# Loads of all lower result parts ahead of group 1's higher part, on the scatters' own semaphores, and TensorE's additions in the order lower parts, then higher parts

## The chip, the cores and the metric

The kernel runs on one core of one Trainium2 chip. The metric is the device time in microseconds (us) of one execution; several executions are timed, and their median is compared. One more execution was taken with the hardware profiler, and all rows below come from it. In what follows SP is the engine that only issues transfers and waits, POOL is GpSimd, DVE is VectorE, ACT is ScalarE and PE is TensorE.

## The reference, cut to what matters

Input `x` has 16 sequences of 256 tokens of 128 numbers: 4096 tokens, 32 tiles of 128 tokens. Two blocks follow each other, each `x = x + s * silu(ffn(xn))`, with `xn = layernorm(x)` and `s` the result of an attention-like layer. Only the end of the second block is touched here:

```
logits = xn @ Wg;  P = softmax(logits);  the two best of 8 experts are kept
h   = gelu(xn @ W1[e] + b1[e])            # 128 -> 512, per expert e
y_e = h @ W2[e] + b2[e]                   # 512 -> 128
y   = sum over the two experts of y_e * P_norm[e]
x   = x + s * silu(y)
```

So each token has two expert results. The one of its expert with the lower number is called its lower part, the other its higher part; `y` is their sum.

## The kernel before, in words

**Groups and units.** The tokens are worked on in 8 groups (0 to 7) of 512. For the second block's experts the rows are routed: POOL scatters every normalised token twice to the DRAM tensor `routed`, sorted by expert, and units of 256 rows of one expert are then read back and multiplied. The first 8 units are the first of each expert (`FIRST_ALL`); the others follow expert by expert, from 0 to 7, in `other_units`. How many there are depends on the data: DVE writes the bounds to `table`, a small row of whole numbers on the chip, and every engine reads them from there (`value_load`, shown in the trace as TENSOR_LOAD with register work behind it). With the reference's inputs the experts get 1096, 830, 727, 1419, 1359, 728, 1148 and 885 rows, which makes 36 units, numbered u0 to u35 here. Expert 6 has its other units in u29 to u32 and expert 7 in u33 to u35.

**What a unit does.** PE turns the unit's rows (L1067), multiplies by W1 (L1077), ACT applies gelu (L1286), PE multiplies by W2 (L1089), DVE adds the bias (L1692), copies the destination rows and weights (L1699, L1702) and multiplies by the weights (L1708). POOL then scatters the 256 result rows in two halves (`scatter`, L739) to the DRAM tensor `results`. There a token's lower part lies in the first 4096 rows and its higher part in the next 4096. The scatters of even units count up the semaphore `y_sent0`, those of odd ones `y_sent1`, by 16 for each half as it lands. In `send_results` POOL issues the first half of unit u, waits until unit u-1 has landed whole (`tell_landing`), counts up `y_landed` (L746), and issues the second half of u. Two others wait for `y_landed`: DVE before it copies the destination rows of unit u (all up to u-2 must have landed), and SP below.

**The end of the kernel on SP.** When the ring of units is loaded, SP reads the results back in 16 loads of 256 KB (`load_results`, L596; 512 tokens by 128 numbers of 4 bytes): 8 lower parts to `res_lower[g]` and 8 higher ones to `res_higher[g]`. Both lie in SBUF room that the program knows by other names: `w_all` (the expert weights) and, for lower part 7, `nT`. Before each load SP reads from `table` how many units must have landed for it (`units_due`, L459) and waits for `y_landed`. With these inputs the numbers are: lower parts 0 to 7: 29, 30, 31, 31, 31, 32, 33, 33; higher parts 0 to 7: 29, 34, 34, 34, 35, 35, 36, 36. (31 means: u30 is the last that must have landed.) The order of the loads is: lower 0, 1, 2, 3, higher 0, 1, lower 4, 5, 6, 7, higher 2, 3, 4, 5, 6, 7. The last two wait for all scatters on `y_sent0` and `y_sent1` directly. Behind the loads, on the same queue, stand the 8 stores of the output (L621), each waiting for its group.

**The end on the other engines.** The parts of groups 0 and 1 are added by DVE (`add_parts`, L1730; `SUMS_BY_DVE = 2`): group 0 ahead of the last unit's bias, group 1 behind the last unit. The parts of groups 2 to 7 are added by PE, as products with a unit matrix that add up in PSUM: for each pair of groups first the two lower parts (L1137, each waiting for its `lower_in`), then the two higher ones (L1140, each waiting for its `res_in`). ACT applies silu group by group (L1317), DVE multiplies by `s` (L1752), adds to `x_all` (L1754), and SP stores. `surplus_results` (L1744) is one small copy that DVE makes behind group 1; it waits for `y_landed` to reach 35.

## Time and profile before

| | us |
|---|---|
| median of 3 runs (lowest, highest) | 445.61 (443.02, 446.01) |
| the profiled execution, its own time | 443.66 |
| its span from the first to the last instruction | 441.9 |
| PE busy in the span | 407.1 (92%) |
| DVE busy | 288.2 (65%) |
| ACT busy | 214.2 (48%) |
| POOL busy | 155.6 (35%) |

The profiled execution is 1.95 us below the median and inside the spread of the three runs; 1.8 us of it lie outside the span. All times below count from the start of the span. "Busy" counts the time in which an engine runs an instruction; the granted clock (PEclk) is the share of full speed that PE was given. A row of the timeline begins with its start and its duration; in square brackets stand the idle time before it and what ended it.

### The profile page before, as it was taken

Reading aid. Unit: us, or ns where it says so; the run is one execution under the profiler, and the core shown is the slowest. Engines: PE = TensorE matmul, PEld = TensorE weight load, DVE = VectorE, ACT = ScalarE, POOL = GpSimd, SP = SyncE. Lnnn points to the kernel's source line nnn. Section 1 sums busy time; section 2 is a strip of 40 time slices with the busy share of each in tenths; the row PEclk is TensorE's granted clock in tenths of the full one; section 3 lists DMA queues with packets and bytes.
Section 4 is the critical chain, followed back from the end, with each engine's and each line's share of the span. In section 5 each row is a group of like instructions: output and inputs, shape, how many; then the busy total and the mean of one; then the engine's idle time right before and its main releaser. Section 6 shows DMA issues by size and latency. Waiting matters only on the chain.

```text
span 441.9 us, 9899 instructions
## 1 busy us (share of the span) xinstructions
PE 407.1 (92%) x2936; PEld 344.5 (78%) x2936; DVE 288.2 (65%) x1149; ACT 214.2 (48%) x525; POOL 155.6 (35%) x215
## 2 busy tenths in 40 slices
PE   8699998999999999999988898889999999999845
PEld 7579777878869779887867788778999999999612
DVE  4889888888888887878866658612433333344445
ACT  3364555556554545542523354323555555555512
POOL 6340015013233250344424002344555555555510
PEclk9999999999999999999999999999999999999969
DMA  7449611244155131131131323321333222223384
GB/s 179 127 111 150 79 40 35 58 151 137 32 159 164 42 87 50 41 90 47 39 86 39 88 52 90 110 70 53 87 85 96 73 71 68 62 73 112 118 297 144
DMA packets 64210, 40.80 MB, mean 92 GB/s; under 512 B 18340, under 2 KB 57128, under 8 KB 64168
## 3 DMA queue, kind: packets, MB, share of 16 engines
q1 hardware_dynamic: 59472, 31.27, 29.5%
q0 software_dynamic: 4352, 8.99, 6.1%
q8 instruction: 21, 0.34, 0.3%
q14 instruction: 21, 0.17, 0.2%
q10 hardware_dynamic: 344, 0.03, 0.1%
HBM read 21.78 MB, written 18.48 MB: 91 GB/s over the span
## 4 chain that ended last, share of the span: by engine, by line
PE 70%; DVE 17%; ACT 5%; issue 4%; DMA 2%; SPq 1%; POOL 0%; DVEq 0%; ACTq 0%; POOLq 0%
PE psA L1077 14%; PE psC L1089 11%; PE psB L903 7%; PE psB L891 5%; PE psB L1100 2%; DVE stats L1375 2%; PE psB L1067 2%; PE psD L1020 2%; DVE nt_a L1390 1%; DVE rstd L1391 1%; DVE nt_a L1389 1%; PE psB L893 1%; PE psD L1003 1%; ACT send L1152 1%; PE psA L849 1%
## 5 line engine op out<-in xcount | busy, mean ns | idle before, releaser
L734 POOL DMA_INDIRECT routed<-send,slot x64 | 64.4, 1006 | 128.0 <-DMA routed<-send,slot 56.4
L739 POOL DMA_INDIRECT results<-nat,y_to x72 | 69.8, 970 | 85.6 <-DVE nat L1708 42.2
L1077 PE MATMUL psA<-xuT,w_all 128*128 128x256 f32 x288 | 68.6, 381 | 1.7 <-ACT h1T L1286 1.0
L1286 ACT ACTIVATE h1T<-psA,b1T 128x256 f32<-128x256 f32 x144 | 63.3, 475 | 8.9 <-PE psB L1100 7.2
L1077 PEld LDWEIGHTS psA<-xuT,w_all 128*128 128x128 f32 x288 | 50.6, 190 | 9.4 <-issue 1.9
L1089 PE MATMUL psC<-w_all,h1T 128*128 128x128 f32 x464 | 56.6, 275 | 0.6 <-ACT h1T L1286 0.6
L1089 PEld LDWEIGHTS psC<-w_all,h1T 128*128 128x128 f32 x464 | 54.1, 192 | 0.8 <-ACT h1T L1286 0.8
L1277 ACT ACTIVATE xuT<-psB 128x256 f32<-128x256 f32 x37 | 14.2, 384 | 62.2 <-PE psB L1067 62.2
L1692 DVE TENSOR_TENSOR nat<-psC,b_all 128x256 f32<-128x256 f32 x29 | 12.3, 425 | 34.3 <-PE psC L1089 34.3
L1680 DVE TENSOR_SCALAR xu<-l_room 128x256 f32 (+1 forms) x38 | 11.3, 298 | 35.7 <-PE psB L1067 25.2
L891 PE MATMUL psB<-xnT,l_room 128*128 128x512 f32 x64 | 34.3, 618 | 0.0
L1217 ACT ACTIVATE hg0T<-psB,b1T 128x512 f32<-128x512 f32 x32 | 22.0, 688 | 22.8 <-PE psB L893 22.7
L903 PE MATMUL psB<-l_room,hg0T 128*128 128x128 f32 x256 | 32.7, 281 | 0.2 <-ACT hg0T L1217 0.2
L903 PEld LDWEIGHTS psB<-l_room,hg0T 128*128 128x128 f32 x256 | 31.2, 192 | 1.1 <-ACT hg0T L1217 0.6
L893 PEld LDWEIGHTS psB<-selT,expert_of 128*128 128x128 bf16 x128 | 9.8, 98 | 18.2 <-issue 18.2
L1708 DVE TENSOR_SCALAR nat<-nat,y_wt 128x128 f32 (+1 forms) x72 | 18.3, 304 | 7.6 <-DVE y_wt L1702 7.4
L794 PE MATMUL psC<-ident 128*128 128x128 f32 x136 | 20.1, 300 | 1.7 <-POOL ident L638 1.7
L1224 ACT ACTIVATE gg<-psB,tok_w 128x128 f32<-128x128 f32 x32 | 9.2, 368 | 25.1 <-PE psB L904 25.1
L794 PEld LDWEIGHTS psC<-ident 128*128 128x128 f32 x136 | 18.6, 214 | 2.3 <-POOL ident L638 1.7
L723 POOL COPY send<-send 128x512 f32<-128x512 f32 x8 | 5.4, 671 | 41.1 <-ACT send L1152 27.9
L1375 DVE BATCH_NORM_STATS2 stats<-x_all 128x6 f32<-128x128 f32 x64 | 13.9, 279 | 5.9 <-DMA x_all<-in_L_attn_x_dram 5.8
L1152 ACT ACTIVATE send<-x_all,shift,rstd 128x128 f32<-128x128 f32 x32 | 13.2, 483 | 8.8 <-DVE shift L1392 8.7
(296 smaller groups left out, 851.9 us busy)
## 6 DMA issues: line engine op xcount, KB each, us to landing
l_room<-routed SPq DMA_DIRECT2D x38, 130.0 KB
inv<-inv_room SPq DMA_DIRECT2D x8, 512.0 KB, 4.1
w_all<-results SPq DMA_DIRECT2D x15, 256.0 KB, 3.8
routed<-blank SPq DMA_DIRECT2D x24, 130.0 KB, 7.5
n_room<-nT SPq DMA_DIRECT2D x8, 256.0 KB, 2.3
w_all<-in_L_ffn_W_dram SPq DMA_DIRECT2D x1, 2048.0 KB, 9.7
out_dram<-x_all SPq DMA_DIRECT2D x8, 256.0 KB, 2.3
results<-nat,y_to POOLq DMA_INDIRECT x72
```

The costliest lines, as they stand in the source:

```text
L734: pool.indirect_dma_start(routed[:, :], bass.IndirectOffsetOnAxis(ap=slot[par][:, c, t:t + 1], axis=0), send[par][:, c, t, :], None).then_ ...
L739: pool.indirect_dma_start(results[:, :], bass.IndirectOffsetOnAxis(ap=y_to[:, par, a:a + 1], axis=0), yw[:, par, a, :], None).then_inc(S[f ...
L794: mm(to, ident[:, :], ident[:, :], start=True, stop=True)
L891: mm(psB[:, j % 2, :], w, xT0[:, :], start=True, stop=False)
L903: mm(o, hg0T[:, j, col(t)], w2_l0[:, j, :], start=(j == 0), stop=False)
L1077: last = mm(psA[:, j // 2, (j % 2) * UNIT:(j % 2 + 1) * UNIT], w1_all[:, e, j * P:(j + 1) * P], xuT[:, :], start=True, stop=True)
L1089: last = mm(psC[:, a, 0:D], h1T[:, k, a * P:(a + 1) * P], w2_all[:, f * JF + k, :], start=(k == 0), stop=(k == JF - 1))
L1152: last = f(to[:, t, 0:D], x_all[:, g * TILES + t, :], ACT.Identity, scale=rstd[:, first + t:first + t + 1], bias=shift[:, first + t:first ...
L1217: f(hg0T[:, j, :], psB[:, j % 2, :], ACT.Gelu, bias=b1T[:, HT + j:HT + j + 1]).then_inc(S["hg0_ready"], 1)
L1286: f(h1T[:, j, :], psA[:, j // 2, (j % 2) * UNIT:(j % 2 + 1) * UNIT], ACT.Gelu, bias=b1T[:, n:n + 1]).then_inc(S["gelu_ready"], 1)
L1375: last = v.bn_stats(stats[:, first + t, :], x_all[:, x_first + t:x_first + t + 1, :])
L1708: last = v.tensor_scalar(yw[:, mine, a, :], yb[:, a:a + 1, :], y_wt[:, a:a + 1], None, ALU.mult)
```

## The change

SP now reads the due counts into registers ahead of the loads (two, then seven, then three in one go), waits for `y_sent0` and `y_sent1` themselves and no longer for POOL's `y_landed`, and issues all other loads in another order: lower 0, 1, 2, 3, higher 0, lower 4, 5, 6, 7, higher 1, 2, 3, 4, 5, 6, 7. PE adds the six lower parts of groups 2 to 7 in a row and then the six higher ones. DVE makes its surplus copy behind group 2.

```
-            last_pair = sp.value_load(table[0:1, 2 * E + 1:2 * E + 2], min_val=MIN_UNITS * E - 2,
-                                      max_val=MAX_UNITS - 1)
...
-            for g in range(groups // 2):
-                wait_on(sp, "y_landed", units_due(sp, g, 0))
+            def wait_landed(units):
+
+                sp.wait_ge(S["y_sent0"], (units + 1) // 2 * (2 * 8 * HALVES))
+                sp.wait_ge(S["y_sent1"], units // 2 * (2 * 8 * HALVES))
+
+            def load_lower(g):
+                wait_landed(low[g])
                 load_results(0, g, res_lower, lower_in)
-            for g in range(SUMS_BY_DVE):
-                wait_on(sp, "y_landed", units_due(sp, g, 1))
+
+            def load_higher(g):
+                wait_landed(high[g])
                 load_results(1, g, res_higher, res_in)
-            for g in range(groups // 2, groups - 2):
-                wait_on(sp, "y_landed", units_due(sp, g, 0))
-                load_results(0, g, res_lower, lower_in)
-            wait_on(sp, "y_landed", bounds[E - 1])
+
+            low = [units_due(sp, g, 0) for g in range(2)]
+            load_lower(0)
+            load_lower(1)
+            low += [units_due(sp, g, 0) for g in range(2, groups - 2)]
+            high = [units_due(sp, g, 1) for g in range(3)]
+            load_lower(2)
+            load_lower(3)
+            load_higher(0)
+            load_lower(4)
+            load_lower(5)
+            high += [units_due(sp, g, 1) for g in range(3, groups - 2)]
+            wait_landed(bounds[E - 1])
             for g in range(groups - 2, groups):
                 load_results(0, g, res_lower, lower_in)
-            for g in range(SUMS_BY_DVE, groups - 2):
-                wait_on(sp, "y_landed", units_due(sp, g, 1))
-                load_results(1, g, res_higher, res_in)
-
-            sp.wait_ge(S["y_sent0"], (last_pair + 2) * (8 * HALVES))
-            sp.wait_ge(S["y_sent1"], (bounds[E] // 2) * (8 * HALVES * 2))
+            for g in range(1, groups - 2):
+                load_higher(g)
+            wait_landed(bounds[E])
             for g in range(groups - 2, groups):
                 load_results(1, g, res_higher, res_in)
...
-            for g0 in range(SUMS_BY_DVE, groups, 2):
-                for g in (g0, g0 + 1):
-                    pe.wait_ge(lower_in[g], 16)
...
-                    mm(sum_ps_of(g), ident[:, :], res_lower[g], start=True, stop=False)
-                for g in (g0, g0 + 1):
-                    pe.wait_ge(res_in[g], 16)
-                    mm(sum_ps_of(g), ident[:, :], res_higher[g], start=False, stop=True).then_inc(S["sum_ps"], 1)
+            for g in range(SUMS_BY_DVE, groups):
+                pe.wait_ge(lower_in[g], 16)
...
+                mm(sum_ps_of(g), ident[:, :], res_lower[g], start=True, stop=False)
+            for g in range(SUMS_BY_DVE, groups):
+                pe.wait_ge(res_in[g], 16)
+                mm(sum_ps_of(g), ident[:, :], res_higher[g], start=False, stop=True).then_inc(S["sum_ps"], 1)
...
             for g in range(groups):
                 finish(g)
-                if g == 1:
+                if g == 2:
                     surplus_results()
```

On PE, behind the last unit's products, the instructions before are these. `lower_in2` is the semaphore of lower part 2's load, `res_in2` that of higher part 2's, and the three tiles psA, psB and psC hold the sums of groups 2 and 3, 4 and 5, and 6 and 7:

```order
L1137 MATMUL psA<-w_all,ident 128x512 [waits lower_in2]
L1137 MATMUL psA<-w_all,ident 128x512 [waits lower_in3]
L1140 MATMUL psA<-w_all,ident 128x512 [waits res_in2]
L1140 MATMUL psA<-w_all,ident 128x512 [waits res_in3]
L1134 REGISTER_ALU [waits lower_in4]
L1137 MATMUL psB<-w_all,ident 128x512 [waits xuT_ready]
L1137 MATMUL psB<-w_all,ident 128x512 [waits lower_in5]
L1140 MATMUL psB<-w_all,ident 128x512 [waits res_in4]
L1140 MATMUL psB<-w_all,ident 128x512 [waits res_in5]
L1137 MATMUL psC<-w_all,ident 128x512 [waits yb_ready,lower_in6]
L1137 MATMUL psC<-nT,ident 128x512 [waits lower_in7]
L1140 MATMUL psC<-w_all,ident 128x512 [waits res_in6]
```

And now, at the same place:

```order
L1146 MATMUL psA<-w_all,ident 128x512 [waits lower_in2]
L1146 MATMUL psA<-w_all,ident 128x512 [waits lower_in3]
L1143 REGISTER_ALU [waits lower_in4]
L1146 MATMUL psB<-w_all,ident 128x512 [waits xuT_ready]
L1146 MATMUL psB<-w_all,ident 128x512 [waits lower_in5]
L1146 MATMUL psC<-w_all,ident 128x512 [waits yb_ready,lower_in6]
L1146 MATMUL psC<-nT,ident 128x512 [waits lower_in7]
L1149 MATMUL psA<-w_all,ident 128x512 [waits res_in2]
L1149 MATMUL psA<-w_all,ident 128x512 [waits res_in3]
L1149 MATMUL psB<-w_all,ident 128x512 [waits res_in4]
L1149 MATMUL psB<-w_all,ident 128x512 [waits res_in5]
L1149 MATMUL psC<-w_all,ident 128x512 [waits res_in6]
```

The four additions of lower parts 4 to 7 have moved ahead of the wait for higher part 2. On SP, the place from the loads of lower part 6 and 7 on reads as follows before:

```order
L596 DMA w_all<-results 128x512 [waits y_landed]
L596 DMA nT<-results 128x512
L459 TENSOR_LOAD table
L459 ISA x2
L409 REGISTER_ALU
L596 DMA w_all<-results 128x512 [waits y_landed]
```

And now:

```order
L594 DMA w_all<-results 128x512 [waits y_sent1]
L594 DMA nT<-results 128x512
L599 ISA
L600 ISA [waits y_sent0]
L594 DMA w_all<-results 128x512 [waits y_sent1]
```

The first row is lower part 6, the last one higher part 2 before and higher part 1 now. The table is no longer read between two loads; two register instructions work out the two counts that are waited for.

## Rows read from the trace of the kernel before

**Rows 1.** Chain of waits near the end (start, duration, what)

```profile
420.65 0.50 POOL results L739
421.16 4.81 DMA w_all<-results
...
426.00 3.71 PE psA L1140 x4
429.71 1.72 PE psB L1137 x4
```

**Rows 2.** POOL's scatters in the timeline, second halves of u31 to u35 (start, duration, instruction)

```profile
407.60 0.97 POOL L739 DMA_INDIRECT results<-nat,y_to  x1 [1.37 <-DMA results<-nat,y_to]
...
411.88 0.97 POOL L739 DMA_INDIRECT results<-nat,y_to  x1 [1.86 <-DMA results<-nat,y_to]
...
414.92 0.97 POOL L739 DMA_INDIRECT results<-nat,y_to  x1 [0.61 <-issue]
...
417.97 0.97 POOL L739 DMA_INDIRECT results<-nat,y_to  x1 [0.30 <-issue]
...
420.65 0.97 POOL L739 DMA_INDIRECT results<-nat,y_to  x1 [0.30 <-issue]
```

**Rows 3.** POOL's announcements of landed units (L746): u31 and u35

```profile
L746 POOLq EVENT_SEMAPHORE  x1: 17/17/17, 411.1 to 411.1; - x1
...
L746 POOLq EVENT_SEMAPHORE  x1: 17/17/17, 426.2 to 426.2; - x1
```

**Rows 4.** SP's loads in the timeline: lower 1, lower 2, higher 1, lower 7, higher 2

```profile
402.49 0.33 SPq L596 DMA_DIRECT2D w_all<-results  x1
...
406.88 0.32 SPq L596 DMA_DIRECT2D w_all<-results  x1
...
417.22 0.32 SPq L596 DMA_DIRECT2D w_all<-results  x1
...
420.07 0.42 SPq L596 DMA_DIRECT2D nT<-results  x1
421.16 0.32 SPq L596 DMA_DIRECT2D w_all<-results  x1
```

**Rows 5.** Issue to landing: higher 0 (408.85), higher 1 (417.22), lower 6 and 7

```profile
DMA to landing us min/median/max: 3.3/3.3/3.3
...
DMA to landing us min/median/max: 2.7/2.7/2.7
...
DMA to landing us min/median/max: 5.1/5.2/5.2
```

**Rows 6.** Stages: start and end, length, busy PE, PEld, DVE, ACT, POOL, clock, DMA share, GB/s

```profile
416.00:417.00 1.00, 1.00 (x10) 0.93 (x9) 0.33 (x2) 0.90 (x3) 0.30 (x1) 1.00 0.20 66
...
422.50:423.00 0.50, 0.00 (x0) 0.00 (x0) 0.47 (x2) 0.00 (x0) 0.00 (x0) 0.68 0.78 299
423.00:425.00 2.00, 0.00 (x0) 0.00 (x0) 0.51 (x2) 0.00 (x0) 0.00 (x0) 0.50 0.99 371
```

**Rows 7.** PE's additions of lower parts 2 and 3, in the timeline

```profile
416.74 1.88 PE L1137 MATMUL psA<-w_all,ident 128*128 128x512 f32 x4
```

**Rows 8.** DVE and ACT: adding the parts of group 1, then groups 6 and 7, in the timeline

```profile
420.02 0.69 DVE L1730 TENSOR_TENSOR w_all<-w_all 128x512 f32<-128x512 f32 x1 [1.43 <-DMA w_all<-results]
...
436.39 0.69 DVE L1752 TENSOR_TENSOR hg0T<-s,hg0T 128x512 f32<-128x512 f32 x1 [0.69 <-ACT hg0T L1317]
436.62 0.60 ACT L1317 ACTIVATE hg0T<-psC 128x512 f32<-128x512 f32 x1 [0.26 <-PE psC L1140]
...
437.73 0.68 DVE L1752 TENSOR_TENSOR hg0T<-s,hg0T 128x512 f32<-128x512 f32 x1
438.44 0.69 DVE L1754 TENSOR_TENSOR x_all<-x_all,hg0T 128x512 f32<-128x512 f32 x1
```

**Rows 9.** DVE around the waits of u33 and u34, in the timeline

```profile
411.52 0.17 DVE L1699 TENSOR_SCALAR y_to<-l_room  x1 [0.54 <-POOLq L746]
...
414.29 0.42 DVE L1692 TENSOR_TENSOR nat<-psC,b_all 128x256 f32<-128x256 f32 x1 [1.13 <-PE psC L1089]
```

More of the change, by code:

```diff
@@ L1128, in _ @@
             other_units(pe, bounds, hid, out)
-            for g0 in range(SUMS_BY_DVE, groups, 2):
-                for g in (g0, g0 + 1):
-                    pe.wait_ge(lower_in[g], 16)
-                    if g == 4:
-                        pe.wait_ge(S["xuT_ready"], bounds[E] + 1)
-                    elif g == 6:
-                        wait_on(pe, "yb_ready", bounds[E])
-                    mm(sum_ps_of(g), ident[:, :], res_lower[g], start=True, stop=False)
-                for g in (g0, g0 + 1):
-                    pe.wait_ge(res_in[g], 16)
-                    mm(sum_ps_of(g), ident[:, :], res_higher[g], start=False, stop=True).then_inc(S["sum_ps"], 1)
+            for g in range(SUMS_BY_DVE, groups):
+                pe.wait_ge(lower_in[g], 16)
+                if g == 4:
+                    pe.wait_ge(S["xuT_ready"], bounds[E] + 1)
+                elif g == 6:
+                    wait_on(pe, "yb_ready", bounds[E])
+                mm(sum_ps_of(g), ident[:, :], res_lower[g], start=True, stop=False)
+            for g in range(SUMS_BY_DVE, groups):
+                pe.wait_ge(res_in[g], 16)
+                mm(sum_ps_of(g), ident[:, :], res_higher[g], start=False, stop=True).then_inc(S["sum_ps"], 1)
         @block.scalar
```

## The prediction

> **What bounds the kernel now.** I read the chain of waits first, from its end, because only work on it can shorten the run. Up to 415 us it is PE's unit products, which the change leaves as they are. From there it is a relay: DVE and POOL finish the last unit, POOL issues its last scatter at 420.65, SP's load of higher part 2 takes 4.81 us from 421.16, and then PE adds without a pause, 3.71 us for the four products of higher parts 2 and 3 and 1.72 us for each later pair [rows 1]. The reader should see two things. PE adds lower parts 2 and 3 from 416.74 to 418.62 [rows 7] and then stands still for 7.4 us in front of higher part 2, although lower parts 4 to 7 stand behind it in its order. And the products at 426.00 take 3.71 us where later ones take 1.72, because the granted clock fell to 0.50 (1.2 GHz) in the pause: it was still 0.68 on average in 422.5 to 423, so it fell some 4 us after the last product [rows 6].
>
> Then SP's timeline: lower part 7 is issued at 420.07 and higher part 2 at 421.16 [rows 4], yet lower 6 and 7 were due when 33 units had landed and higher part 2 at 34, which SP had seen at 417.22 when it issued higher part 1. Nine loads thus stand in a row from 417.2 on (higher 1, lower 4 to 7, higher 2 to 5), just when the last scatters have to land, and the 16 transfer engines are 0.99 busy at 371 GB/s [rows 6]. Loads take 5.1 to 5.2 us there instead of 2.7 [rows 5], and u35's second half, issued at 420.65, is announced only at 426.2 [rows 2, 3]: 5.5 us, where u33's, issued at 414.92, had moved all its data by 417.0 [rows 2, 6], 2.1 us, in a window with 66 GB/s.
>
> **Part 1: reading the counts ahead.** A read and a load together take 1.09 us (421.16 less 420.07); the load alone 0.42 [rows 4], so a read costs at most 0.67. Seven reads, 4.7 us, now stand between lower part 1 (402.49) and lower part 2 (406.88) [rows 4], in a gap of 4.4 us in which SP waited. So lower part 2 comes at about 407.6, 0.7 late, which nobody waits for: PE needs it at 416.7. Three more reads (2.0 us) stand ahead of lower part 6 and are covered by the wait for u32. In front of the last higher parts no read is left: between 0.42 and 1.09 us from load to load, and I take 0.6, nearer to 0.42, as two register instructions remain.
>
> **Part 2: the semaphores.** Waiting for the landing itself saves only what POOL was late in telling. For u33 at most 0.2 us (417.0 against 417.22). For u34, whose second half was issued at 417.97 [rows 2], the telling waits until POOL has issued u35's second half at 420.65 and comes at 421.16; direct, it is due at 420.1 with 2.1 us, or 421.5 with the 3.5 us that u31's took beside three loads (407.60 to 411.1 [rows 2, 3]). A gain of up to 1.1 for higher parts 4 and 5, which is on the path only if they are late.
>
> **Part 3: the loads moved forward.** Lower 4 and 5 move to about 409.4 and 411.5, lower 6 and 7 to about 414.4 and 415.0, when u32 has landed. Each is 256 KB, 0.7 us of all transfer engines at 371 GB/s. That is bought from the scatters now in flight there. Bounds for u33: landing at 417.0 if nothing is lost; 1.4 later if both loads are served wholly first. I take 1.0 later, nearer to the upper end because POOL itself will run some tenths later behind u31 and u32: higher part 1 at 418.0, 0.8 later than before. Its own landing is between 2.7 and 3.3 us (a load with two others close by [rows 5]); I take 3.3, since higher 2 and 3 follow within 1.2 us: 421.3.
>
> The Trainium skill, page "DMA: Bandwidth & Descriptors", section "Issuing engines are not separate DMA queues", speaks against this part: transfers started by SP and by GpSimd end up on the same 16 engines and interleave. The sum by that rule alone would give back the time of every load moved into the scatters' stretch; the rows agree so far that u31's landing took 3.5 us beside loads and u33's 2.1 without.
>
> **Part 4: PE's order.** Six lower additions in a row, 1.88/2 = 0.94 us each at most [rows 7], or 0.86 by the chain: from 416.74 to 421.9 or 422.4. Lower 7 has landed by 415.0 + 3.3. Higher part 2, issued at 418.6, lands between 3.3 and 3.6 us later, at about 422. So PE has hardly a pause, keeps 2.4 GHz, and each higher part costs 0.86 us when it lands. Off PE's path go 7.4 us of standing still, less the waits for single parts.
>
> **Part 5: what is late next.** DVE. It adds the parts of group 1 once higher part 1 has landed (before at 420.02 [rows 8]), and then owes eight groups of two instructions: 436.39 to 437.73 is 1.34 us, 437.73 to 439.13 is 1.40 [rows 8], so 1.37 each. Before, six of these eight waited for PE; now they stand in a row. The surplus copy, at nothing before because DVE was waiting anyway, is now in this row: I take 0.3, between the 0.17 us of its like [rows 9] and one instruction of 0.69. DVE starts at 421.4, 0.65 for group 1's sum, 8 x 1.37 = 11.0, 0.3: **433.3**, against 439.13. The last store and the end behind it, 2.8 us, stay.
>
> Does the last group come in time? POOL: u34's second half was issued 0.75 after u33's landing was told, u35's 2.68 later [rows 2]; so 418.8 and 421.5. At 3.5 us u35 has landed at 425.0. Higher 7 is issued at 425.5 and lands, with 3.8 (between 3.3 and 4.8), at 429.3; PE 0.86, ACT 0.60: 430.8. DVE turns to group 7 at 431.9. It fits by 1.1 us.
>
> **Sum.** 439.1 - 433.3 = 5.8 us less. The profiled execution took 443.66 (span 441.9), which makes 437.9. It lay 1.95 below the median of the runs; from the median the sum gives 439.8. I put the time between the two, at **438.8 us**, with the span of a profiled execution at 436.1.
>
> **Rivals.**
>
> A. *DVE's row, as above.* Bounds: higher part 1 neither later nor slower, DVE's end 431.9, a gain of 7.2; or all ends at their worst, higher part 1 at 418.6 and 3.6 us to land, a gain of about 4.8. Chance 0.60.
>
> B. *PE falls back to 1.2 GHz between the higher parts.* Behind higher 3 PE waits for u34 and u35, twice some 2 us. For: it fell in the pause of 7.4 us. Against: it took some 4 us of standing still. Then the four products of a pair take 3.71 us: higher 6 ends at 430.9, higher 7 at 432.7, ACT 433.3, DVE 434.7. A gain of 4.4 us, time about 440.2. Chance 0.13. The Trainium skill, page "TensorE: Matmul & The Clock Gate", section "Loop structure matters more than you think", warns of a DMA wait between matmuls in this way: by it PE would go to half its clock. The trace agrees for the one long pause; it has no pause of 2 us here to judge by.
>
> C. *The scatters pay for the loads.* Every landing from u31 to u33 stretches by 1 to 1.4 us, not only u33's; POOL waits for each, so higher part 1 comes at about 420.2 and lands at 423.5, and DVE's row of 12 us ends at 435.5; u35 at about 428 gives much the same end. A gain of 3.6 us, time 441.0. For: u31's 3.5 us. Against: the last scatter meets five loads fewer. Chance 0.15.
>
> D. *The change doesn't do what it says:* lower parts 4 to 7 still land late and PE's wait only changes its place. Against: their counts are reached by 414.4. What remains is PE's clock, a gain of some 2 us (3.71 less 1.72 [rows 1]), time 442.6. Chance 0.04.
>
> E. *Slower.* The stretch runs back into the units. DVE already waited 0.54 us for the telling of u31 (ended 411.1) at 411.52, and has 1.13 us to spare before the bias of u34 at 414.29 [rows 9]. If the landings of u31 to u35 all take 3.5 us and add what they wait for, u35 is issued 6 us later; PE's last products, 2 us late beyond the spare 1.1, follow; higher 7 lands at 434.5 plus 3, and DVE ends at 437.5 + 0.86 + 0.60 + 1.4 = 440.4, which is 1.3 us later than before: 446 us, and more if the loads behind them slow down too. It decides once a scatter's landing is stretched by over 1.1 us at u32. Against: each load is only 0.7 us. Chance 0.08.
>
> **Range and chances.** Low end: A's best case from the profiled time, 436.4. High end: C's 441.0 and, since I stand between two levels 1.9 us apart, 1.3 more: 442.3. What lies outside is E, D in part and A's luckiest tail. A measurement here tells 1% (4.5 us) from no change. Faster by over 1%: A's 0.60 and half of B, 0.66. Within: the rest of B, C, D and half of E, 0.29. Slower by over 1%: 0.05.
>
> **What would show it.** Right: lower 4 to 7 issued before 415.5; PE's six lower additions in one piece from 416.7; DVE without a gap from group 1's sum to its last instruction, 12 us; u35's second half landed in under 4.5 us; granted clock 1.00 in the higher additions. Wrong: DVE waiting for ACT at groups 6 and 7 (B, or late landings); higher part 1 issued after 418.6 (C); the bias of u34 later than 414.5 (E).

## The result and the profile after

The changed kernel takes 439.44 us (median of 8 runs, 438.9 to 441.46); the kernel before, run beside it, 445.45 us (8 runs). The ratio, which is one of means, is 0.9875, with a 95% interval of 0.9849 to 0.9901: 5.6 us faster (6.0 between the two medians). I had put the gain at 5.8 and the time at 438.8. The profiled execution took 438.9 us, its span is 437.1. Ratios, here and below, leave out slow executions, of which one chip had four (480 to 1435 us); the medians given for that chip (before 452.39) count them.

The gain is where it was looked for. PE's additions in the timeline of the changed kernel (start, duration, instruction; in brackets the idle time before it and what ended it; L1146 adds lower parts, L1149 higher parts):

```profile
418.15 1.88 PE L1146 MATMUL psA<-w_all,ident 128*128 128x512 f32 x4
419.87 1.88 PE L1146 MATMUL psB<-w_all,ident 128*128 128x512 f32 x4
421.59 1.02 PE L1146 MATMUL psC<-w_all,ident 128*128 128x512 f32 x2
422.45 1.02 PE L1146 MATMUL psC<-nT,ident 128*128 128x512 f32 x2
423.31 1.88 PE L1149 MATMUL psA<-w_all,ident 128*128 128x512 f32 x4
426.42 1.98 PE L1149 MATMUL psB<-w_all,ident 128*128 128x512 f32 x4 [1.23 <-DMA w_all<-results]
429.39 1.98 PE L1149 MATMUL psC<-w_all,ident 128*128 128x512 f32 x4 [0.98 <-DMA w_all<-results]
```

Six lower parts go by in one piece from 418.15 to 423.3, and the pause of 7.4 us [rows 1, 7] has become two of 1.23 and 0.98. No row of four products takes more than 1.98 us; before, the first such after the pause took 3.71 [rows 1]. The granted clock is 1.00 from 415 to 433.

DVE's row in the timeline, from the sum of group 1's parts to its last instruction:

```profile
421.81 0.69 DVE L1739 TENSOR_TENSOR w_all<-w_all 128x512 f32<-128x512 f32 x1 [1.36 <-DMA w_all<-results]
422.42 0.68 DVE L1761 TENSOR_TENSOR hg0T<-s,hg0T 128x512 f32<-128x512 f32 x1
...
426.41 0.16 DVE L1753 TENSOR_SCALAR y_to<-fill 128x2 int32 x1
426.48 0.69 DVE L1761 TENSOR_TENSOR hg0T<-s,hg0T 128x512 f32<-128x512 f32 x1
...
428.21 0.69 DVE L1761 TENSOR_TENSOR hg0T<-s,hg0T 128x512 f32<-128x512 f32 x1 [0.32 <-ACT hg0T L1326]
...
431.18 0.69 DVE L1761 TENSOR_TENSOR hg0T<-s,hg0T 128x512 f32<-128x512 f32 x1 [0.22 <-ACT hg0T L1326]
...
433.23 0.69 DVE L1763 TENSOR_TENSOR x_all<-x_all,hg0T 128x512 f32<-128x512 f32 x1
```

The row is nearly full: 12.1 us with two waits for ACT, before groups 4 and 6. The surplus copy moves what follows it by 0.07 us (426.41 to 426.48).

The chain of waits says what ends those waits. Near the end it reads (start, duration, what):

```profile
422.51 4.05 DMA results<-nat,y_to
...
426.58 2.76 DMA w_all<-results
...
429.39 1.14 PE psC L1149 x2
...
430.55 0.61 ACT hg0T L1326
...
431.18 0.70 DVE hg0T L1761
```

From the issue of u35's second half at 422.51 nothing is spare: its landing, the load of higher part 6, one addition, one silu, and then DVE's last four instructions. Before, the chain's DMA in that place was the load of higher part 2, of 4.81 us [rows 1].

**Where the traces must not be laid over each other by the clock on the wall.** In this execution PE's last unit product ends at 418.32, before at 416.90. The cause lies 400 us earlier. Windows of the changed kernel (busy of PE, PEld, DVE, ACT, POOL, granted clock, DMA share, GB/s):

```profile
20.00:22.00 2.00, 1.73 (x6) 1.09 (x7) 1.97 (x10) 1.37 (x5) 1.73 (x7) 0.70 0.00 0
22.00:24.00 2.00, 2.00 (x9) 1.26 (x8) 1.70 (x7) 1.97 (x4) 1.87 (x7) 0.50 0.04 8
```

Before, both windows show 1.00. The code there is the same, and the dip comes and goes: of 14 profiled executions, 7 have it, with one and the same kernel on either side. In the ten traces that were not taken on the chip with 452.39 us, PE's last unit product ends at 418.1 to 418.9 with the dip and at 416.4 to 417.3 without it. So I use two measures: the ratio of the runs, and the *tail*, from the end of PE's last unit product to DVE's last end. The tail is 22.23 us before and 15.61 in this execution, 6.6 less. A second profile of the changed kernel (the run `e9_changed_again` below) has no dip, its last unit product ends at 416.95, and its tail is 16.94, 5.3 less. A tail isn't free of the dip either: where PE is late and something else is last, the tail is short by PE's lateness, so tails are compared with the dip in mind. This second trace can be laid over the one of before, and most of the points below are read there.

### The profile page after: what moved, and what is told of

Read it like the earlier page. It is cut to its first block, busy times and chain, and to the rows that moved or that the text cites. A ratio compares the mean times of both kernels' runs of the same rounds, so it can differ in the third digit from the quotient of the medians.

```text
span 437.1 us, 9909 instructions
## 1 busy us (share of the span) xinstructions
PE 407.2 (93%) x2936; PEld 345.0 (79%) x2936; DVE 287.8 (66%) x1149; ACT 214.3 (49%) x525; POOL 155.6 (36%) x215
## 4 chain that ended last, share of the span: by engine, by line
PE 60%; DVE 16%; issue 9%; DMA 6%; ACT 4%; POOL 3%; SPq 1%; POOLq 0%; DVEq 0%; ACTq 0%
PE psA L1087 13%; PE psC L1099 11%; PE psB L913 6%; PE psB L901 5%; POOL routed L744 2%; DMA routed<-send,slot 2%; PE psB L1110 2%; DVE stats L1384 2%; PE psB L1077 2%; DMA results<-nat,y_to 2%; PE psD L1030 2%; PE psC L804 1%; PE psB L903 1%; DVE nt_a L1398 1%; DVE nt_a L1399 1%
## 5 line engine op out<-in xcount | busy, mean ns | idle before, releaser
L901 PE MATMUL psB<-xnT,l_room 128*128 128x512 f32 x64 | 35.3, 634 | 0.0
L804 PE MATMUL psC<-ident 128*128 128x128 f32 x136 | 21.1, 309 | 1.7 <-POOL ident L648 1.7
```

The costliest lines, as they stand in the source:

```text
L804: mm(to, ident[:, :], ident[:, :], start=True, stop=True)
L901: mm(psB[:, j % 2, :], w, xT0[:, :], start=True, stop=False)
```

## Experiments

Each is told with its edit, and "before" in it means the kernel before on the same chip. The first four shared one chip (before 444.99 us, 14 runs), the next four another (452.39, 12 runs), the last four a third (445.24, 11 runs).

### PE's order alone: e1_pe_order_only

The kernel before, with the new order of PE's additions and nothing else.

```diff
-            for g0 in range(SUMS_BY_DVE, groups, 2):
...
+            for g in range(SUMS_BY_DVE, groups):
+                pe.wait_ge(lower_in[g], 16)
...
+            for g in range(SUMS_BY_DVE, groups):
+                pe.wait_ge(res_in[g], 16)
```

> Only PE's order is changed (six lower additions, then six higher ones); SP's loads, their waits and reads, and the surplus copy stay as before. If PE standing still in front of higher part 2 is half of the loss: PE adds lower 4 to 7 as they land (421.4 to 425.3 us in the trace of before) and is free when higher 2 lands at 426.0, at 2.4 GHz; six higher additions of 0.86 us, last one behind the landing of higher 7 at 430.7; DVE then needs six groups of 1.37 us from 427.7 and ends at 435.9 where it ended at 439.1. Gain 3.2 us, ratio to before 0.993. If the order of the additions is worth nothing without the earlier loads: ratio 1.000.

Measured: 443.16 us (9 runs), ratio 0.9955 [0.9931, 0.9978], a gain of 2.0; tail 19.99. It lies between the two expectations. Its PE (L1136 lower, L1139 higher):

```profile
417.10 1.88 PE L1136 MATMUL psA<-w_all,ident 128*128 128x512 f32 x4
422.40 3.56 PE L1136 MATMUL psB<-w_all,ident 128*128 128x512 f32 x4 [3.42 <-DMA w_all<-results]
...
427.52 1.88 PE L1139 MATMUL psA<-w_all,ident 128*128 128x512 f32 x4
```

Lower parts 4 and 5 are still loaded behind higher part 1, so PE waits 3.42 us for them and its clock falls all the same, at the end of the wait (0.71 on average in 422.0 to 422.5, then 0.50; 3.56 us for four products). The order alone only shifts the pause; it is paid while loads are outstanding anyway. Higher part 2, next in PE's order, is added at 427.5 instead of 426.0.

### The loads alone: e2_sp_only

The changed kernel with PE's old order, by pairs.

```diff
-            for g in range(SUMS_BY_DVE, groups):
+            for g0 in range(SUMS_BY_DVE, groups, 2):
+                for g in (g0, g0 + 1):
+                    pe.wait_ge(lower_in[g], 16)
...
+                for g in (g0, g0 + 1):
+                    pe.wait_ge(res_in[g], 16)
```

> The changed kernel with PE's order of before (pair by pair). If what binds now is the landing of the last loads and DVE's row, PE's order costs nothing: with the landings of the changed kernel's trace (higher 2 at 422.4, 4 at 426.4, 6 at 429.3) the pairwise order ends higher 6 at 430.7 against 430.5, so the time is that of the changed kernel plus 0.2 us, ratio to before 0.988. If the pause in front of higher 2 (2.4 us here) drops PE's clock to 1.2 GHz, every addition takes 1.85 us and the end moves by some 2 to 3 us: ratio 0.993 to 0.995, and granted clock 0.5 in 423 to 427.

Measured: 440.87 us (6 runs), ratio 0.992 [0.9892, 0.9949], a gain of 3.6; tail 18.75. Its PE (L1150 higher, L1147 lower) and its windows:

```profile
422.34 3.40 PE L1150 MATMUL psA<-w_all,ident 128*128 128x512 f32 x4 [3.87 <-DMA w_all<-results]
425.54 2.27 PE L1147 MATMUL psB<-w_all,ident 128*128 128x512 f32 x4
```

```profile
422.00:422.50 0.50, 0.16 (x1) 0.16 (x2) 0.50 (x2) 0.22 (x1) 0.20 (x2) 1.00 0.73 270
422.50:424.00 1.50, 1.50 (x3) 0.47 (x4) 1.47 (x3) 0.47 (x2) 1.20 (x1) 0.63 0.40 152
424.00:425.50 1.50, 1.50 (x2) 0.51 (x2) 1.47 (x3) 0.55 (x1) 0.00 (x0) 0.50 0.58 188
```

The pause is half of what it was, but the clock still falls, and here it falls *after* PE has begun again: 1.00 until 422.5, then 0.63 and 0.50 (1.2 GHz). The work that had been waiting pays for the pause.

### The pause filled: e6_filled

The same kernel with 14 idle products into a bank of PSUM that nothing reads, between lower 3 and higher 2. They add nothing to the result.

```diff
+                if g0 == SUMS_BY_DVE:
+                    idle_products(FILLERS, psD[:, 0, 0:P])
```

> The run with SP's part alone (PE adds pair by pair, ratio 0.992 to before, higher 2 and 3 added at granted clock 0.5, 3.40 us for the four products) and 14 more products of 128 columns on PE into an unused PSUM bank in the pause in front of higher part 2. The sums are as before. If PE's new order is worth what it keeps of the clock: the clock stays 1.00, the four products take 1.9 us and the time is that of the changed kernel, ratio 0.988. If the order itself matters (lower 4 to 7 standing in front of higher 6): the clock stays up and the ratio stays at 0.992.

Measured: 446.73 us (6 runs) where before takes 452.39, ratio 0.9882 [0.9841, 0.9923]; tail 15.98, against 18.75 without the filler.

```profile
424.87 3.29 PE L805 MATMUL psD<-ident 128*128 128x128 f32 x28
428.00 1.88 PE L1153 MATMUL psA<-w_all,ident 128*128 128x512 f32 x4
```

The additions behind it go at 1.88 us per four, and the clock is 1.00 from 423 to 433. With the clock kept, PE's old order can't be told from the new one by these runs. What the new order is worth, on top of the loads, is the clock that it keeps. This rests on the clock and the tails, which are from two traces without the dip; the two ratios, 0.992 and 0.9882, were taken on different chips and their intervals overlap.

### Is DVE's row the bound? e3_finish0_first and e4_dve_quiet

In the first, DVE finishes group 0 (whose parts are long there) before it adds the parts of group 1, which takes 1.3 us of work out of the row behind higher part 1. In the second it starts the row only when all units have been told.

```diff
+            finish(0)
             for g in range(1, SUMS_BY_DVE):
                 add_parts(g)
-            for g in range(groups):
+            for g in range(1, groups):
```

> The changed kernel, but DVE multiplies and adds group 0 before it adds the parts of group 1, in the 1.36 us in which it waits for higher part 1. Theory of the prediction (DVE's row of 12 us sets the end): everything behind moves forward by 1.3 us, 438.1 us against 439.4. Rival (the landing of the last unit and the loads of higher 6 and 7 set the end; groups 4 and 6 wait for them): DVE only waits longer ahead of group 4 (by 1.3) and the end stays, 439.4 within 0.3.

```diff
             dve.wait_ge(S["s1_ready"], groups)
+            wait_on(dve, "y_landed", bounds[E])
```

> The changed kernel, but DVE stands still from the last unit until all units are told as landed, and only then adds the parts of group 1 and does its row. It will be slower; what is looked at is the last scatter. In the changed kernel u35's second half takes 1.43 us on POOL instead of 0.97 and lands 4.05 us after its issue, with the transfer engines idle for a good part of it. If DVE's instructions with two SBUF inputs hold POOL up: 0.97 us on POOL and 2.1 to 2.6 us to landing; span about 440.5. If it is the transfers of higher 1 to 5 beside it: still about 4 us to landing; span about 442.

The first measured 439.64 us (6 runs), ratio 0.9869 [0.9841, 0.9898]: no gain over the changed kernel. Its DVE:

```profile
423.41 0.69 DVE L1739 TENSOR_TENSOR w_all<-w_all 128x512 f32<-128x512 f32 x1
424.80 0.69 DVE L1761 TENSOR_TENSOR hg0T<-s,hg0T 128x512 f32<-128x512 f32 x1 [0.70 <-ACT hg0T L1326]
...
429.88 0.69 DVE L1761 TENSOR_TENSOR hg0T<-s,hg0T 128x512 f32<-128x512 f32 x1 [0.95 <-ACT hg0T L1326]
```

The two waits have different causes. The first, 0.70 us, comes with the edit: ACT begins its silu of group 1 at 424.14, when DVE's sum is there, and DVE has nothing to do meanwhile, since group 0 is done. So the row became only 0.6 us shorter. The second, 0.95 us ahead of group 4, is for ACT, which waits for a late higher part. So the row is not the only bound, though this experiment tests it with half the force that it was meant to have. The second, one run of 442.54 us with a span of 440.8, shows the row by itself: from 426.66 to 438.04 without a gap, 11.4 us. In the changed kernel a row of 11.4 us from 421.81 would end at 433.2; it ended at 433.92. Two paths lie within 0.7 us of each other. The second run also answers the question it was made for: with DVE at rest u35's last scatter took 0.97 us on POOL instead of 1.43 and landed after 2.24 us instead of 4.05. The second trace of the changed kernel, further down, has 0.97 and 2.05 with DVE at work; there the two instructions started together (see the last section).

### The order without the semaphores: e5_order_only

The kernel before with the new order of loads and of additions, but still waiting for what POOL announces, and with a read of the table ahead of each load.

```diff
+            def load_due(c, g):
+                wait_on(sp, "y_landed", units_due(sp, g, c))
...
             for g in range(groups // 2):
-                wait_on(sp, "y_landed", units_due(sp, g, 0))
-                load_results(0, g, res_lower, lower_in)
...
+                load_due(0, g)
+            load_due(1, 0)
             for g in range(groups // 2, groups - 2):
...
+            for g in range(1, groups - 2):
+                load_due(1, g)
```

> The kernel before with the changed order of SP's loads and of PE's additions alone: SP still waits for POOL's y_landed and reads each count just ahead of its load. If the change lives on the order of the loads and additions, and the semaphores and the reading ahead are worth under 0.5 us (u33 and u34 are told as soon as they land, since POOL is waiting for them): ratio to before 0.988, 439.6 us. If the direct semaphores carry part of it (up to 1.1 us for the loads of higher 4 to 7) and the reads of 0.6 us between higher 1 and 5 delay group 4: ratio 0.992.

Measured: 446.87 us (6 runs) against 452.39, ratio 0.9857 [0.9817, 0.9897]; tail 15.12. The order alone gives the whole gain; for the reads ahead and the scatters' own semaphores nothing is left that these runs can tell from zero. The changed kernel's trace says why: higher part 4, which waits for u34, is issued at 423.58, just when POOL announces u34 (423.5). The landing is what both wait for. (This trace has the dip, which makes its tail short.)

### Loads beside the scatters: e7_lower67_late and e8_tell_behind

The first loads lower parts 6 and 7 behind higher part 1, out of the way of u33's scatters. In the second POOL issues both halves of a unit before it waits for the unit ahead.

```diff
-            wait_landed(bounds[E - 1])
+            load_higher(1)
             for g in range(groups - 2, groups):
                 load_results(0, g, res_lower, lower_in)
-            for g in range(1, groups - 2):
+            for g in range(2, groups - 2):
```

> The changed kernel with lower parts 6 and 7 loaded behind higher part 1. It puts a price on the loads beside u33's scatter: with them u33's second half took 3.0 us to land (two traces of the changed loads), without them 2.1 in the trace of before. If the loads stretch it: about 2.1 us here, higher 1 issued 0.9 us earlier measured from PE's last unit product. If the scatter's landing is long for another reason: still 3.0. The time should be that of the changed kernel within 0.7 us, since lower 6 and 7 now come late for PE.

```diff
                 scatter(par, 0)
+                scatter(par, 1)
                 if behind:
                     tell_landing(u - 1, 1 - par)
-                scatter(par, 1)
```

> The changed kernel, but POOL issues both halves of unit u before it waits for unit u-1 to land and tells it. In the traces of the changed loads POOL waited for a landing between the halves, and u35's second half was issued 4.2 to 6.0 us after PE's last unit product. If that wait passes the stretched landings on to the end: issued at 3.4 to 4.2 us in this trace, and 0.5 to 1 us less in the median, 438.6. If POOL and DVE only wait elsewhere (DVE for the later telling): 439.4 within 0.3.

The first: 445.31 us (4 runs), ratio 0.9836 [0.9796, 0.9877], tail 15.93. From u33's second half to the load of higher part 1 it is 2.27 us, against 3.0 in the changed kernel and 2.57 to 3.28 in the others with the two loads beside it; before, it was 2.30. The two loads cost u33 0.3 to 1.0 us. But u34 then meets them: from its second half to the load that waits for it are 4.56 us, where the changed kernel has 3.8. The ratio is the lowest of all runs here, but its interval covers that of the changed kernel, so a gain over it isn't shown.

The second: 445.57 us (6 runs), ratio 0.9847 [0.9815, 0.9879], tail 14.89, the shortest of all. u35's second half goes out 3.48 us after PE's last product instead of 4.19 and 5.49 in the two traces of the changed kernel. But in the trace of `e6_filled`, where POOL tells as before, it goes out after 3.59, and the trace of this run has the dip. So neither number shows what telling later is worth, and by the runs it can't be told from the changed kernel.

### The changed kernel again, and a hold on DVE: e9_changed_again and e10_hold

> The changed kernel once more, beside the three below on one chip, so that they can be compared with it. Both theories: ratio to before 0.984 to 0.990; from PE's last unit product to DVE's end 15 to 17 us.

439.36 us (6 runs) against 445.24, ratio 0.9865 [0.9814, 0.9915], span 436.6. The gain is the same in this second set of runs. Its chain of waits from u30's second half on:

```profile
403.06 4.42 DMA results<-nat,y_to
...
408.26 3.85 DMA results<-nat,y_to
...
412.89 0.71 POOL results L749
...
415.93 3.01 DMA results<-nat,y_to
...
418.96 0.02 POOLq L756
...
419.72 0.71 POOL results L749
...
422.44 2.05 DMA results<-nat,y_to
...
424.76 4.55 DMA w_all<-results
...
429.35 1.14 PE psC L1149 x2
430.49 0.02 issue
430.51 0.61 ACT hg0T L1326
...
431.14 0.70 DVE hg0T L1761
```

PE's unit products, which filled the same stretch of the chain before, are gone from it. (In the first trace of the changed kernel they fill it up to 411.95.) POOL waits for u30, then u31 (3.85 us beside the loads of lower 2 to 4 and higher 0), then u33 (3.01), before each next second half. Against before, where PE's products end at the same time, higher part 1 is due at 418.96 instead of 417.22 [rows 3, 4], 1.74 later, and u35's second half is 1.8 later (422.44 and 420.65 [rows 2]). Not all of this is the price of the loads. Before, u30's second half was issued and told here (POOL's timeline, then L746):

```profile
403.21 0.97 POOL L739 DMA_INDIRECT results<-nat,y_to  x1 [0.50 <-issue]
L746 POOLq EVENT_SEMAPHORE  x1: 17/17/17, 406.8 to 406.8; - x1
```

It took 3.6 us, and 4.42 now, although no load that changed its place in the order had been issued yet. So u31's second half began 0.66 us later (408.26 and 407.60 [rows 2]) which no moved load can have caused; in `e1_pe_order_only`, with the loads of before, it began later still, at 408.89. Then u31 took 3.85 us instead of 3.5 [rows 2, 3], and u33 3.03 up to the load instead of 2.30: 0.35 and 0.73 are what can be put down to the loads. The first trace bears this out: measured from PE's last unit product, higher part 1 is issued 0.70 us behind it there, against 0.32 before and 2.01 here. The relay's lateness also explains why the dip did not lengthen that execution: PE was 1.4 us late, and DVE ended at 433.92, here at 433.89; the two tails, 15.61 and 16.94, differ by PE's lateness alone.

In the hold, DVE begins its last row only when POOL has issued u35's second half, because a scatter that starts while DVE reads two operands of SBUF takes longer (see the last section).

```diff
             send_results(last_pair + 1, 1, False)
+            pool.sem_inc(S["last_issued"], 1)
...
             dve.wait_ge(S["s1_ready"], groups)
+            dve.wait_ge(S["last_issued"], 1)
```

> The changed kernel, but DVE begins its last row (the parts of group 1 and all behind) only when POOL has issued the second half of u35, some 0.5 us after that instruction's start. If what stretches the last scatter is a DVE instruction with two SBUF inputs that already runs when POOL's starts: POOL's instruction takes 0.97 us and its half lands 2.3 to 2.9 us after its issue, although DVE then works on without a pause. If it is DVE's work beside the transfer, or the loads: about 4.0 us as before. The end: DVE's row of 12 us begins later, so 0.5 to 1 us slower than the changed kernel.

440.46 us (4 runs), ratio 0.9898 [0.9842, 0.9954], tail 17.23: no gain. The scatter took 0.97 us and the load behind it was issued 2.47 us after it, but this load, of higher part 6, then took 4.3 us, where it took 2.76 in the changed kernel's first trace. The second trace of the changed kernel has the same pair without any hold (2.05, then 4.55), so it can't be put down to the hold. And PE shows something that had not come up (PE, then windows):

```profile
424.70 1.13 PE L1150 MATMUL psA<-w_all,ident 128*128 128x512 f32 x2 [0.56 <-DMA w_all<-results]
427.05 3.57 PE L1150 MATMUL psB<-w_all,ident 128*128 128x512 f32 x4 [1.22 <-DMA w_all<-results]
```

```profile
425.50:427.00 1.50, 0.33 (x1) 0.00 (x0) 1.47 (x3) 0.60 (x1) 0.00 (x0) 1.00 0.94 303
427.00:430.70 3.70, 3.65 (x5) 1.54 (x6) 2.65 (x6) 0.64 (x2) 0.00 (x0) 0.54 0.99 287
```

The clock fell after pauses of 0.56 and 1.22 us, where the second trace of the changed kernel has 0.36 and 1.31 at the same place, and that of `e3_finish0_first` 0.39 and 1.45, and both keep it. So this trace says little about the hold, and it shows that with the order of the change the clock can still fall.

### Put together: e11_combined and e12_order_tell_behind

The first gives group 1 to PE, finishes group 0 first, holds DVE and tells behind both halves.

```diff
-SUMS_BY_DVE = 2
+SUMS_BY_DVE = 1
...
                 scatter(par, 0)
+                scatter(par, 1)
                 if behind:
                     tell_landing(u - 1, 1 - par)
-                scatter(par, 1)
...
+            pe.wait_ge(S["s1_ready"], groups)
...
+            finish(0)
+            dve.wait_ge(S["last_issued"], 1)
+            for g in range(1, groups):
```

> Both limits moved at once, for a kernel that beats the changed one: group 1's parts are added by PE, DVE finishes group 0 first and then holds until POOL has issued u35's second half, and POOL tells landings behind both halves. Landing of u35 2.3 to 2.9 us after issue; DVE's row behind the hold is 7 groups, 9.6 us. If both limits were the two that bind: from PE's last unit product to DVE's end 14.8 us or less, 0.5 to 1 us less than the changed kernel. If something else binds: the same as the changed kernel.

439.41 us (6 runs), ratio 0.9864 [0.9823, 0.9906], tail 17.05 where 14.8 or less was expected: not better. PE now has seven lower parts ahead of group 1's higher part and comes to it at 422.90, 5.8 us after its last unit product; DVE stands still from 420.3 to 424.66, and its row from there to 434.11 has no gap. I had moved the bound onto PE's queue.

The second is the order alone together with telling behind both halves.

```diff
                 scatter(par, 0)
+                scatter(par, 1)
                 if behind:
                     tell_landing(u - 1, 1 - par)
-                scatter(par, 1)
```

> The kernel before with the changed order of loads and additions alone and with POOL telling landings behind both halves of a scatter, SP waiting for y_landed. If the direct semaphores matter once POOL tells later (SP would see u33 and u34 up to 1 us later): 0.5 to 1 us slower than the changed kernel. If not: within 0.3 us of it.

438.75 us (6 runs, 436.99 to 439.41), ratio 0.9847 [0.9803, 0.9891], tail 16.23 without the dip. It is the lowest median on its chip, and needs neither the semaphores nor the reads ahead, but its interval covers that of the changed kernel beside it (0.9865 [0.9814, 0.9915]). It beats the kernel before; that it beats the change isn't shown.

## Why the prediction was right

The mechanism was right and so was the sum. Its terms were not all right, and two errors met. I judge them by the second trace, whose PE ends with the one of before.

- **Part 1, reads ahead.** I had lower part 2 at 407.6; it was issued at 407.6 in both traces. The reads turned out to be worth nothing either way (e5).
- **Part 2, the semaphores.** I had "a gain of up to 1.1 for higher parts 4 and 5, which is on the path only if they are late". The runs can't tell it from nothing: u34 landed so late (told at 423.5) that POOL had begun its last scatter 1 us before, at 422.44, and nothing was left to be late in telling.
- **Part 3, the loads forward.** Lower 6 and 7 came at 415.3 and 415.7, 0.9 and 0.7 late. Higher part 1 was to come 0.8 later than before, and came 1.74 later (due at 418.96). The price of the loads was about right: 1.0 for u33 and "some tenths" for u31 and u32 forecast, 0.73 for u33 and 0.35 for u31 measured. What I did not have is that the relay can start late by itself: 0.66 us came with u30, ahead of every load that moved, and in the first trace there was nothing of it. Higher part 1 in turn landed in 2.7 us, not 3.3, as it had before [rows 5].
- **Part 4, PE's order.** Right: six additions in one piece, 0.86 us each, clock 1.00 in both traces. Experiments e2 and e6 show that the clock is what this order brings.
- **Part 5, DVE's row.** The length was 11.4 us (e4) where I had 11.95: a pair takes 1.33 us, not 1.37, and the surplus copy 0.07, not 0.3. The start was 421.82 against my 421.4. So the row alone ends at 433.2, as forecast at 433.3, out of a later start and a shorter row.
- **"It fits by 1.1 us."** This step failed. I compared the last half with group 7 only. Higher parts 6 and 7 go out together, PE works them one after the other, and the tight group is 6: DVE waits 0.31 us before it in the second trace and 0.22 in the first, which I had named as a sign of being wrong ("DVE waiting for ACT"). The waits around groups 4 and 6 made up the 0.7 us by which the row ended behind 433.2. The landings were not worse than forecast: from u35's second half to the landing of higher part 6 it took 6.9 us (2.05 + 4.55 and 0.3 between), where I had 7.8 for higher part 7 and it was 7.5. Late was the issue: 422.44 where I had 421.5. Hence e3, which gave DVE 0.6 us, brought nothing that the runs can tell.

Of the rivals, A held for the likeliest end. C's sign, higher part 1 issued after 418.6, is there in both traces, and u35's second half is 1.8 us later than before in the second. But its mechanism, every landing stretched by 1 to 1.4 us, is not: they stretched by 0.35 and 0.73. In the first trace the sign is there because PE itself was 1.4 us late. The later start of DVE's row moved the end little because the faster landing of higher part 1 (0.6) had kept it down and the shorter row (0.55) paid for it. That these errors cancelled is luck. B did not happen in either trace of the changed kernel; e10 shows that it can, at about the price I gave (3.57 us for four products). D fell with the timeline of PE. E's sign, the bias of u34 later than 414.5, was there in the first trace (415.70), but only by the dip at 20 us; in the second it came at 414.34. The end was 0.6 us later than forecast in DVE's last instruction (433.9 and 433.3) and 0.5 later in the span (436.6 and 436.1).

The second rule that I had weighed, that transfers started by SP and GpSimd share the same 16 engines (the Trainium skill, "DMA: Bandwidth & Descriptors", "Issuing engines are not separate DMA queues"), is borne out by u33: 3.0 us up to the load behind it beside the two loads, against 2.30 before and 2.27 in e7 without them. The price by these rows is 0.3 to 1.0 us for each landing on the relay, not the full time of the loads. Of the clock, the Trainium skill, page "TensorE: Matmul & The Clock Gate", section "Loop structure matters more than you think", warns of long DMA waits between matmuls; the traces agree for pauses of 3.42 and 3.87 us, and disagree with each other for those of 1.2 to 1.5.

What stays open: why one trace of the changed kernel has 3.2 us behind DVE's last instruction and the other 2.7, and what makes u31's second half start 1.7 us earlier against PE in one trace of the changed kernel than in the other. No experiment took the loads of lower 2 to 4 out of u31's way, so the 0.35 us by which it took longer than before is read from single traces, not shown by an edit.

## What to carry to other kernels

When loads and an engine's additions each stand in an order, look at both: either alone left PE waiting and let its clock fall, with 2.0 and 3.6 us of gain, and the two together gave 5.6. That is their plain sum; nothing here shows that one needs the other. When a forecast rests on one engine's full row, check each of the last groups against its own arrival, not only the last one. When a relay of landings is priced by one trace against another, see first how far the same relay moves between executions of unchanged code. Before a trace is laid over another, find a common event upstream of the change: a dip 400 us away had moved everything by 1.4 us.

## What the runs showed of the hardware

**A scatter that starts while DVE reads SBUF in certain ways takes longer.** A scatter of POOL that started 0.07 to 0.24 us into a DVE instruction with two SBUF inputs took 1.29 to 1.45 us instead of 0.97. In the changed kernel (POOL, timeline):

```profile
421.24 0.97 POOL L749 DMA_INDIRECT results<-nat,y_to  x1 [0.49 <-issue]
422.51 1.43 POOL L749 DMA_INDIRECT results<-nat,y_to  x1 [0.30 <-issue]
```

DVE's instruction ran from 422.42 to 423.10 and the scatter ended at 423.94, 0.84 us after it. In all traces with such an overlap (seven other kernels here) it is 0.83 to 0.85. It looks as if the scatter could not end earlier than that: one that started 0.51 us into the instruction took 1.03 (e7), and those that started with some 0.1 us of it or less to go kept their 0.97. Where POOL was first, and where both started within 0.02 us, the scatter kept its 0.97; DVE's instruction took 0.69 in the first case and 0.69 to 0.75 in the second. The same is seen with DVE's copy of a unit's rows, which has one SBUF input, in five overlaps (here before, POOL and DVE):

```profile
401.65 1.06 POOL L739 DMA_INDIRECT results<-nat,y_to  x1 [0.88 <-DVE nat L1708]
401.58 0.29 DVE L1680 TENSOR_SCALAR xu<-l_room 128x256 f32 x1 [0.71 <-PE psB L1067]
```

It is not seen with the adding of the bias, which takes one input from PSUM: a scatter that started 0.06 us into such an instruction of 0.42 us kept its 0.97 (e3, at 416.01). The Trainium skill, page "SBUF — State Buffer", section "Who interferes with whom", has it that a DVE instruction with two SBUF inputs contends with a GpSimd instruction that reads SBUF and that issue order decides who is blocked. The rows agree where DVE was first; where POOL was first they show no delay of DVE. Where u35's last scatter was delayed beside the new loads, it had landed after 3.95 to 4.1 us, otherwise after 2.1 to 3.4 (mostly counted up to the load behind it). Mostly the load behind it evened that out: higher part 6 took 2.6 to 2.8 us after the late landings and 3.7 to 4.6 after most of the early ones.

**TensorE's clock can fall in the pause or in the work behind it.** Before, it fell in the pause, some 4 us after the last product and 3 us ahead of the next [rows 6]. In `e1_pe_order_only` it was 0.71 on average in 422.0 to 422.5, after 3.42 us of standing still that ended at 422.40. In `e2_sp_only` it was 1.00 through the pause of 3.87 us and for the first tenths of the products behind it, then 0.63 and 0.50 in the windows up to 425.5. In `e10_hold` it fell behind two pauses of 0.56 and 1.22 us, while it stayed at 1.00 behind 1.23, 1.31 and 1.45 in three other traces.

**A dip far from any change.** At 20 to 24 us, where PE comes back to work after a long pause, half of the 14 profiled executions fall to 0.50 and half do not. It is worth 1.4 us at PE's end.
